# Feed-forward inner sum in two column tiles, output bias added by an accumulating DMA

## The reference

```
mod = (silu(c) @ wmod)                       # per batch: sa, ca, ga, sb, cb, gb
h = layernorm(x) * (1 + ca) + sa
x = x + ga * state_space(h)                  # projections, a scan over time with 16 states, projection, layernorm
h = layernorm(x) * (1 + cb) + sb
s = h @ Win + bin                            # 512 -> 64
hid = relu(s[..., None] * W1 + b1)           # 64 x 16
g = sum over the 16 of (hid * W2) + b2       # 64: the inner sum
x = x + gb * (g @ Wout + bout)               # 64 -> 512
```

## Time and profile before

| | |
|---|---|
| time, median of 3 runs | 4576.69 us |
| lowest and highest | 4574.44 and 4577.13 us |
| the profiled execution | 4574.68 us |
| its span, first to last instruction | 4572.9 us |
| mean granted TensorE clock | 0.990 of full speed |
| TensorE busy | 4356.8 us, 95% |
| VectorE, ScalarE, GpSimd busy | 3698.9, 3814.2, 3596.2 us |
| one repeat in the middle | 138.7 us |

### The profile page before, as it was taken

How to read it: one execution, slowest core, us unless ns; L and a number is a source line. 1 busy time by engine, 2 the same in 40 slices (tenths; PEclk the granted TensorE clock), 3 DMA queues, 4 the chain that set the end, 5 groups by cost and what they waited for, 6 DMA issues and landing times. The chain is left out here.

```text
span 4572.9 us, 69933 instructions
## 1 busy us (share of the span) xinstructions
PE 4356.8 (95%) x22528; PEld 2784.8 (61%) x22528; DVE 3698.9 (81%) x5132; ACT 3814.2 (83%) x6371; POOL 3596.2 (79%) x1999
## 2 busy tenths in 40 slices
PE   7999999999999999999999999999999999999997
PEld 3666666666666666666666666666666666666664
DVE  3778888888888888888888888888888888888885
ACT  3788888888888888888888888888888888888885
POOL 3787878887878877877878878878788878788784
PEclk8999999999999999999999999999999999999999
DMA  4233233333233333332333333332333333333322
GB/s 138 73 79 87 81 89 82 85 81 88 80 94 81 83 88 87 85 87 77 86 93 83 89 82 84 83 90 78 91 76 89 87 86 86 86 77 89 86 77 58
DMA packets 177763, 388.89 MB, mean 85 GB/s; under 512 B 22693, under 2 KB 22693, under 8 KB 177402
## 3 DMA queue, kind: packets, MB, share of 16 engines
q1 hardware_dynamic: 140538, 250.19, 17.4%
q0 software_dynamic: 36864, 134.23, 15.3%
HBM read 215.50 MB, written 34.63 MB: 55 GB/s over the span
## 5 line engine op out<-in xcount | busy, mean ns | idle before, releaser
L379 POOL TENSOR_TENSOR work<-work,c_bc 128x1024 f32<-128x1024 f32 x1024 | 2463.3, 2418 | 765.9 <-DVE work L1140 676.7
L1140 DVE TENSOR_TENSOR_SCAN work<-work,state,b_ps 128x512 f32<-128x512 f32 x1792 | 2257.7, 1274 | 301.1 <-PE b_ps L468 272.7
L852 ACT ACTIVATE work<-u_td,b_td 128x512 f32<-128x512 f32 x2048 | 1453.2, 710 | 163.7 <-PE b_ps L468 158.3
L842 ACT ACTIVATE work<-dt_t,neg_a 128x512 f32<-128x512 f32 x2048 | 1451.3, 709 | 4.7 <-DVE work L1140 4.4
L468 PE MATMUL b_ps<-ident,work 128*128 128x128 f32 x8192 | 1253.3, 276 | 65.0 <-DVE work L1140 57.1
L468 PEld LDWEIGHTS b_ps<-ident,work 128*128 128x128 f32 x8192 | 974.8, 142 | 505.3 <-issue 303.2
L543 PEld LDWEIGHTS y_ps<-ident,work 128*128 128x128 f32 x6144 | 740.0, 142 | 481.7 <-issue 466.0
L543 PE MATMUL y_ps<-ident,work 128*128 128x128 f32 x6144 | 862.8, 273 | 1.6 <-DMA work<-work 1.3
L692 PE MATMUL dense<-h_t,w_in_t 128*128 128x512 f32 x1024 | 514.5, 599 | 1.1 <-DVE u_td L1223 1.1
L600 PE MATMUL dense<-w_out_t,proj 128*128 128x512 f32 x1024 | 509.9, 595 | 0.0
L658 PE MATMUL dense<-xs_t,w_dt_t 128*128 128x512 f32 x1024 | 501.2, 593 | 0.0
(11 more groups left out here) (115 smaller groups left out, 4530.4 us busy)
## 6 DMA issues: line engine op xcount, KB each, us to landing
c_bc<-c_d SPq DMA_DIRECT2D x512, 256.0 KB, 3.3
work<-work POOLq DMA_DIRECT2D x256, 512.0 KB, 5.6
xn<-in_x SPq DMA_DIRECT2D x128, 256.0 KB, 5.1
x<-in_x SPq DMA_DIRECT2D x128, 256.0 KB, 4.3
out_dram<-x SPq DMA_DIRECT2D x128, 256.0 KB, 4.4
work<-in_wmod SPq DMA_DIRECT2D x2, 1024.0 KB, 6.5
w_in_t<-in_w_in_t SPq DMA_DIRECT2D x2, 1024.0 KB, 9.9
gain_shift<-par_d SPq DMA_DIRECT2D x8, 256.0 KB, 6.0
```

The lines of the kernel that those rows point to most:

```text
L379: gp.tensor_tensor(made_here, both(hs, HS_RING, s * U + i), c_bc[:, (s * N + n) % C_RING:(s * N + n) % C_RING + 1, :].to_broadcast([P, 2, ...
L842: A(decay[:, (s * U + i) % DEC_RING, :], dt_t[:, s % 2, j, :], ACT.Exp, scale=neg_a[:, j, n:n + 1]).then_inc(S["dec_done"], 1)
L852: A(v[:, n % V_RING, tb, :], u_td[:, tb, :], ACT.Copy, scale=b_td[:, s % 2, tb, n:n + 1]).then_inc(S["v_done"], 1)
L1140: V.tensor_tensor_scan(hs[:, (s * U + i) % HS_RING, :], decay[:, (s * U + i) % DEC_RING, :], b_ps[:, i % 2, :], state[:, i:i + 1] if s % N ...
```

## The change

- The 8 g matmuls become 16. The weight w2_dg is 128 x 64. Tokens 0 to 255 go to rows 0 to 63 of the bank, tokens 256 to 511 to rows 64 to 127, by column tiles at 0 and 64. gm is then 128 x 256.
- The 4 out matmuls read 64 rows of gm and of wout_g, the upper or the lower half of the array (row tiles at 0 and 64); Wout is loaded to both halves, and b2 too.
- The row of ones for bout is gone. The bias times its gate goes to a fourth row set of par_d at the start, and once per chunk GpSimd issues a DMA that adds it, spread to 128 partitions and four blocks, into x1 (add_bout), after the second normalization has read x1. VectorE waits for it before it adds out.
- The zeroing of padded weights and one mask go, with the waits for them.

```diff
-        w2_dg = sb("w2_dg", [P, J, P])
+        w2_dg = sb("w2_dg", [P, J, M])
...
-            load("late_loaded", wout_b[0:M, :], ap["Wout"])
-            load("late_loaded", wout_b[M:M + 1, :], row("bout"))
-            sp.wait_ge(S["const_masks"], 2)
-            load("b2_loaded", b2[0:M, :], column("b2"))
+            for h in range(2):
+                load("late_loaded", wout_b[h * M:(h + 1) * M, :], ap["Wout"])
+                load("b2_loaded", b2[h * M:(h + 1) * M, :], column("b2"))
...
+                load("bout_row", bout_r, row("bout").to_broadcast([B, D]))
...
+                sp.wait_ge(S["bout_made"], 1)
+                sp.dma_start(par_d[3], bias_r).then_inc(S["par_stored"], Q)
...
+            def add_bout(b):
+                yield SECOND[TB - 1] + 2 + TB + 1
+                gp.wait_ge(S["par_stored"], 4 * Q)
+                gp.wait_ge(S["xn2_done"], at("xn2_done", b, TB))
+                gp.dma_start(x1[:, :, :], par_d[3:4, b // NC:b // NC + 1, :].to_broadcast([P, TB, D]),
+                             accum_op=ALU.add).then_inc(S["bout_added"], Q)
...
-                mm(long(s, "g")[:, :], w2_dg[:, k, :], tmp[:, k % RELU_RING, :], start=(k == 0), stop=(k == J - 1)
-                   ).then_inc(S["g_used"], 1)
+                for h in range(2):
+                    last = mm(long(s, "g")[h * M:(h + 1) * M, 0:T // 2], w2_dg[:, k, :],
+                              tmp[:, k % RELU_RING, h * (T // 2):(h + 1) * (T // 2)], start=(k == 0), stop=(k == J - 1),
+                              tile_position=(0, h * M))
+                last.then_inc(S["g_used"], 1)
...
-                mm(to[:, :], gm[:, tb * P:(tb + 1) * P], wout_g[:, :], start=True, stop=True).then_inc(S["out_ps"], 1)
+                h = tb // 2
+                mm(to[:, :], gm[h * M:(h + 1) * M, tb % 2 * P:(tb % 2 + 1) * P], wout_g[h * M:(h + 1) * M, :], start=True,
+                   stop=True, tile_position=(h * M, 0)).then_inc(S["out_ps"], 1)
...
-                A(gm[:, :], long(s, "g")[:, :], ACT.Identity, bias=b2[:, :]).then_inc(S["gm_done"], 1)
+                A(gm[:, 0:T // 2], long(s, "g")[:, 0:T // 2], ACT.Identity, bias=b2[:, :]).then_inc(S["gm_done"], 1)
...
+                yield 21
+                dve.wait_ge(S["bout_row"], Q)
+                V.tensor_tensor(bias_r, bout_r, gate_b, ALU.mult).then_inc(S["bout_made"], 1)
...
                     dve.wait_ge(S["out_ps"], at("out_ps", c, tb + 1))
+                    dve.wait_ge(S["bout_added"], (c + 1) * Q)
```

More of the change, by code:

```diff
@@ L97, in pb @@
             return ctx.enter_context(nc.psum_tensor(name, shape, f32))
-        par_d = nc.dram_tensor("par_d", (3, B, D), f32).ap()
+        par_d = nc.dram_tensor("par_d", (4, B, D), f32).ap()
         c_d = nc.dram_tensor("c_d", (2, N, T), f32).ap()
@@ L164, in build_program @@
         gamma_r, beta_r, gain_r, shift_r = (dt_t[0:B, 1, n, :] for n in range(4))
+        bout_r, bias_r = (x1[0:B, n, :] for n in range(2))
         y_ps = pb("y_ps", [P, TB, D])
@@ L179, in build_program @@
         w2dg_done b_out_loaded bout_done moved_ps moved c_exp c_one c_rcp silu_c rows_ps rows_taken mods_ps mods_done sign_done gate_done par_made
-        par_stored gs_loaded wg_loaded wout_done""".split()
+        par_stored bout_row bout_made bout_added gs_loaded wg_loaded wout_done""".split()
         PER = {
@@ L256, in _ @@
             load("wx_loaded", b_in[:, :], ap["b_in_c"])
-            sp.wait_ge(S["const_zeroed"], 5)
             load("wd_loaded", w_dt[:, :, :], blocks("w_dt_t"))
@@ L286, in store_gates @@
                 sp.dma_start(par_d[1], shift_r).then_inc(S["par_stored"], Q)
+                sp.wait_ge(S["bout_made"], 1)
+                sp.dma_start(par_d[3], bias_r).then_inc(S["par_stored"], Q)
             def load_gain(k):
                 if k == 0:
-                    sp.wait_ge(S["par_stored"], 3 * Q)
+                    sp.wait_ge(S["par_stored"], 4 * Q)
                 sp.wait_ge(S["x1_done"], at("x1_done", k, 0))
@@ L350, in _ @@
             count_up(gp, "Pool")
[L351 to L361, removed]
+            gp.memset(ident[:, :], 0.0).then_inc(S["const_zeroed"], 1)
+            gp.wait_ge(S["const_zeroed"], 1)
+            gp.affine_select(out=ident[:, :], in_=ident[:, :], compare_op=ALU.not_equal, fill=1.0, base=0,
+                             pattern=[[-1, P]], channel_multiplier=1).then_inc(S["const_masks"], 1)
             def both(ring, of, i):
@@ L444, in step @@
                 if has_b:
-                    chains += [last_gate(b), attended(b)]
+                    chains += [last_gate(b), attended(b), add_bout(b)]
                 if has_b and b % NC == 0:
@@ L886, in feed_forward @@
                 yield made("g", J - 1)
-                act.wait_ge(S["b2_loaded"], Q)
+                act.wait_ge(S["b2_loaded"], 2 * Q)
                 act.wait_ge(S["g_used"], at("g_used", c, J))
                 act.wait_ge(S["rel_done"], at("rel_done", c, J))
-                A(gm[:, :], long(s, "g")[:, :], ACT.Identity, bias=b2[:, :]).then_inc(S["gm_done"], 1)
+                A(gm[:, 0:T // 2], long(s, "g")[:, 0:T // 2], ACT.Identity, bias=b2[:, :]).then_inc(S["gm_done"], 1)
             def skip(s):
@@ L1115, in late_modulation @@
                                        ).then_inc(S["scal_done"], 1)
-                dve.wait_ge(S["const_zeroed"], 3)
                 dve.wait_ge(S["const_masks"], 1)
@@ L1126, in late_modulation @@
                 last.then_inc(S["w2dg_done"], 1)
+                yield 21
+                dve.wait_ge(S["bout_row"], Q)
+                V.tensor_tensor(bias_r, bout_r, gate_b, ALU.mult).then_inc(S["bout_made"], 1)
                 yield 25
-                dve.wait_ge(S["par_stored"], 3 * Q)
+                dve.wait_ge(S["par_stored"], 4 * Q)
             def scan(s, i):
```

## The result

| | median | lowest to highest | runs |
|---|---|---|---|
| before | 4575.97 us | 4574.05 to 4577.13 | 9 |
| changed | 4589.57 us | 4572.96 to 4590.80 | 9 |

The ratio is 1.0025, with a 95% interval of 1.0015 to 1.0035: slower by 13.6 us between the medians, 11.5 between the means. The profiled execution of the changed kernel took 4584.85 us around a span of 4583.1, 10.2 us more than that of before. The times spread more than before's 3 us, and the spread turns out to be part of the answer.

A forecast was written before the change was run, and what follows sets the result against it. TensorE was taken to set the pace except in a piece led by VectorE; -0.35 us a repeat over thirty gave -10, the tail -1.5, so 4565 us median, own case 4560 to 4571 (45%), whole range 4551 to 4606.

The forecast's parts named there:

- no two records overlap: Rival on the column tiles: bursts and out.2 only pay for shape changes, +0.93 us a repeat, 4605 us; chance 28%.
- the larger chance on faster: Chances given for the measured outcome: 0.43 faster, 0.24 within about 9 us of no change, 0.33 slower.
- The step that failed: Second piece of a repeat, led by VectorE: changes there go into TensorE's 2.3 us of waits, not the repeat.
- this piece: Second of four pieces of a repeat, 20.3 us long, VectorE busy 19.7 and TensorE waiting 2.3 us.
- What bounds the kernel: TensorE, busy 95%, sets the repeat's pace except in the second piece; savings in the two head bursts shorten the repeat.
- The column tiles: Inner-sum bursts of two g: 2n+1 steps of 0.215 us, 1.08 in place of 1.72, 0.64 us saved a burst.
- all pair up: Rival on the column tiles: 0.86 us saved a burst, -0.79 us a repeat, 4552 us; chance 12%.
- The change of shape: Price of switching tile shape and back on TensorE: 0.29 us a burst, 0.35 us for each out.
- out.3 covered by the wait of 0.58: At out.3, its 0.35 us shape change was to be hidden in TensorE's 0.58 us wait before 2205.93.
- The sum of a repeat: Two head bursts at -0.64 + 0.29 make -0.70, out.2 adds 0.35: -0.35 us a repeat, -10 us over thirty.
- The DMA: GpSimd's added issue per chunk taken as 2 us, landing in 6 to 11 us, all of it hidden.
- The tail: The eight g matmuls alone at the end, paced by ScalarE's relus: 8.1 us becomes 6.6, -1.5 us.

The follow-up runs named there:

- the run with the filler: Changed kernel plus one full-array matmul of zero weights added to pre.1's sum just before out.1, where TensorE waits: 4561.50 us, ratio 0.9969.
- one column tile: Column-tiled sum with outs in the full array, both token halves of the sum sent to the same column tile: 4595.88 us, ratio 1.0045 to before.
- the kernel before with row tiles: Kernel before with the bias by accumulating DMA and outs reading 64 rows as row tiles, inner sum untouched: 4610.99 us, ratio 1.0078.
- The full-array version: Changed kernel with the four outs back in the full array, zero-padded weights held twice; column tiles and DMA stay: 4540.63 us, ratio 0.9923 to before.
- a shorter sum alone: Kernel before with the eight g products reading only the first 256 of 512 tokens, no tiles: 4542.22 us, ratio 0.9927.
- the DMA alone: Kernel before with the output bias added by the accumulating DMA, inner sum and outs unchanged: 4577.61 us, ratio 1.0004.
- both runs without the DMA: Changed kernel without the accumulating DMA, output bias left out, run twice: 4575.20 and 4578.78 us, ratios 1.0001 and 1.0006 to before.

## Why the prediction was right and wrong

The range of 4551 to 4606 us held the 4589.57, but by luck: its upper end came from "no two records overlap", which the trace excludes. The forecast of 4565 and the larger chance on faster missed the sign.

**The step that failed** is "g.4 to g.7, out.0 and out.1 lie in this piece: what changes there changes these waits, not the repeat". It let the row tile at out.1 stand at nothing, and took TensorE's clock as given. What the runs showed in its place: behind out.1 the granted clock falls to 0.50 in 15 of 29 repeats of the profiled execution, 1.69 us each, 25 us in all, and 28 us by the run with the filler. The repeat without falls went the way that was forecast. Point by point:

- **What bounds the kernel: right.** The bursts at the head come off the repeat, VectorE had the room, and g.3 did not wait for ScalarE.
- **The column tiles: the term was mis-sized.** It was taken from "records of different tiles overlap while those of one tile follow each other", 2n+1 steps. Measured: 2n steps, 0.85 saved a burst and not 0.64. The rival "all pair up" named this, with 12%. The Trainium skill, "TensorE: Matmul & The Clock Gate", Part 3, gives about 4 ns a tile on top of one matmul's duration; the trace agrees in kind, with 7 ns between the two of a pair.
- **The change of shape: right.** 0.29 a burst predicted, 0.30 measured in one column tile. The "TensorEngine Tiling (Array Packing)" page of the Trainium skill, Tiling Modes, says that a change of mode drains the engine. The trace agrees as far as that each change has a price; no run here parts a drain from the rest of the 0.30. An out as a row tile: 0.35 predicted; 0.35 measured for out.2, and 0.34 in the kernel before with row tiles.
- **out.3 covered by the wait of 0.58: wrong.** TensorE's next step in that chain waits for two: ScalarE's xn, which the profile names, and VectorE's step L1198 on pre.2. In the trace of before they end together: ScalarE at 2205.88, VectorE at 2205.79, TensorE starts at 2205.93.

VectorE before:

```profile
2205.04 0.75 DVE L1198 SCALAR_TENSOR_TENSOR tmp<-dense,norm,gain_shift 128x512 f32<-128x512 f32 x1
```

ScalarE and VectorE after, which end at 2203.32 and 2203.56, with TensorE's start at 2203.66 (the profile still names ScalarE):

```profile
2202.52 0.80 ACT L919 ACTIVATE xn<-xn,norm 128x512 f32<-128x512 f32 x1
```

```profile
2202.81 0.75 DVE L1208 SCALAR_TENSOR_TENSOR tmp<-dense,norm,gain_shift 128x512 f32<-128x512 f32 x1
```

  VectorE's chain hangs on pre.2, which out.3 delays. Its cover was 0.09 us (2205.79 to 2205.88), not 0.58, and of its 0.35 out.3 cost 0.26 a repeat. The prediction had named this as what would be wrong if the wait were gone; the wait stayed, and that hid it.
- **The sum of a repeat: nearly right by two errors that cancel.** -0.70 + 0.35 = -0.35 predicted; 2 x (-0.86 + 0.30) + 0.35 (out.2) + 0.26 (out.3) = -0.51, and -0.51 measured. The bursts gave 0.42 more than their term and out.3 took 0.26 that it was not charged. The full-array version, which has neither of the last two, has -1.12.
- **The DMA: right on its own terms.** 2 us of issue taken, 1.64 measured; 6 to 11 us of landing, 10.8 measured; nothing waits. Its part in the number of falls was not foreseen.
- **The tail: right.** -1.5 predicted, -1.6 measured from the first relu to the last g; of the whole stretch from the last repeat's start to the end, 0.95 came off.
- **The clock: missing.** No term, no rival. The rows of before held the place: TensorE with waits of 0.83 and 0.53 on either side of out.1, into which the change put a product that fills half of the array's rows. With the falls at 1.7 each, some 16 of them, a gain of 14.5 us (4575.97 to the 4561.50 with the filler) became a loss of 13.6.

**Shown:** the falls behind out.1 come with the row tile there (one product changed brings them), and not with the waits alone, a shorter sum alone, or the DMA alone; filling the wait ends them, and so does the full-array form.

**Open, first:** whether it is the half-empty rows or the change of shape itself that counts for the clock, for each row tile here has both. The changed kernel's own trace speaks for the rows: g.7, a change of shape to 64 columns with all 128 rows in use, stands between waits of 0.53 and 0.66 us, in a stretch where TensorE is less busy (1.90 of 3.40 us) than ahead of the falls (2.18 of 3.40), and there is no fall behind it in any repeat.

```profile
923.00:926.40 3.40, 1.90 (x13) 1.07 (x13) 3.40 (x6) 3.40 (x7) 2.10 (x2) 1.00 0.14 49
```

```profile
925.08 0.65 PE L555 MATMUL dense<-tmp,w_dg 128*64 128x256 f32 x4
926.40 0.63 PE L600 MATMUL dense<-ident,h_t 128*128 128x128 f32 x4 [0.66 <-DVE proj L1187]
```

So a change of shape among waits is not enough by itself. No run has a row change with all rows at work, so this is not settled.

**Open, second:** why only some repeats are hit, and how the DMA raises their number. In the changed kernel falls come in rows 139.9 to 140.0 us apart, which is the length of a disturbed repeat, so that one fall puts the next repeat's out.1 at the same distance. In the kernel before with row tiles a disturbed repeat lasts 140.9 us, and its falls never stand in neighbouring repeats (280 us apart at least). The rows begin and end in the same repeats in both runs without the DMA (1628.3 to 2048.1 and 1630.2 to 2050.1 us). This points to the moment at which a repeat reaches out.1, which a small shift changes. It was not tested further.

## What to carry to other kernels

Two column tiles halve the streaming of a small stationary even in float32, for 0.30 us a burst to the new shape and back; a lone product gains nothing in a row tile, and here the same product in the full array with zero-padded weights was the better form: 0.77% faster than before, where the change as made was 0.25% slower. A product that lies within waits is free only as long as the clock holds, and a busy share that stays the same doesn't promise that it will: look at the granted clock after an edit has put a row tile into such a stretch. And where a step waits for several engines, the cover of a delay is the slack of the engine that the delay goes through, not the wait that the profile shows.

## What the runs showed of the hardware

- Records of two column tiles start 7 ns apart and both float32 records of each pair up: 4 steps of about 0.22 us for two matmuls of 2 x 256 columns, 1.02 us against 1.87 in one tile.
- A change from the full array to 64 columns and back costs 0.30 us in a stream of float32 matmuls, 0.25 of it before the next product and the rest in it; a row tile of 64 rows and 512 columns 0.34 to 0.35, where nothing covers it.
- TensorE's granted clock fell to 0.50 for 3.4 us behind a row tile of 64 rows that stood between waits of 0.84 and 0.39 us. It did not behind the full-array product between waits of 0.83 and 0.53, at an equal or smaller busy time, nor behind a tile of 64 columns between waits of 0.53 and 0.66. Each fall cost 1.7 us.
- It also fell in three profiled executions behind a wait of 2.08 to 2.11 us among full-array products, and did not behind the same wait of 2.12 in the kernel before.
- The changed kernel's time has a grain of 1.7 us, the number of falls, which differs from run to run (4570.15 us with 5, 4586.85 with 17).
- An accumulating DMA of 1 MB from a repeated row of 2 KB holds GpSimd for 1.64 us and lands in 10.8 us.
